# A graph network kernel: one gathered tile of every 64 moved from GpSimd to ScalarE's queue in three of six passes

## The reference

```python
h = relu(layernorm(x)); x = x + [(1 + eps) * h + segment_sum(h[src] * edge_weight, dst)]       # L0
h = relu(layernorm(x)); x = x + L1(h)   # h = relu(h @ W_node + b); 3 times: m = h @ conv[i],
                                        # agg = segment_sum(w_e * m[src], dst), h = GRU(agg, h)
h = relu(layernorm(x)); x = x + L2(h)   # segment_sum(alpha[rel] * (h @ w_rel)[src], dst) + ..., relu
h = relu(layernorm(x)); x = x + L3(h)   # (h + mean over src of h[dst]) @ W.T + b
```

## Time and profile before

| | us |
|---|---|
| median of 3 runs | 6545.01 (6538.51 to 6546.88) |
| profiled execution | 6555.57, of which the span is 6553.8 |
| POOL busy | 4766.0 (73%) |
| DVE busy | 3827.2 (58%) |
| PE busy | 3315.8 (51%) |
| ACT busy | 858.8 (13%) |

### The profile page before, as it was taken

The page is one execution under the profiler, slowest core; times in us unless marked ns, Lnnn a source line. Parts: engine busy times, 40 slices in busy tenths (PEclk is TensorE's granted clock), DMA queues, the critical chain, the costliest instruction groups (busy, mean ns, idle before and its releaser), DMA issues.

```text
span 6553.8 us, 107755 instructions
## 1 busy us (share of the span) xinstructions
PE 3315.8 (51%) x13560; PEld 2693.6 (41%) x13560; DVE 3827.2 (58%) x13371; ACT 858.8 (13%) x2167; POOL 4766.0 (73%) x5006
## 2 busy tenths in 40 slices
PE   3444445444447555555755554696444444444444
PEld 3333334333334444444444543343333333333333
DVE  6767666666666656656666664454454444444445
ACT  1000001000002111111211110143333333000000
POOL 6777776777774677777677777675777776777775
PEclk9555556555557666666876665696555555555556
DMA  5434442333332222222122222154222222222222
GB/s 140 111 107 110 110 110 74 74 75 75 75 75 53 53 54 54 54 54 53 46 54 53 53 54 54 48 212 140 54 53 54 53 54 55 54 54 54 54 54 59
DMA packets 276003, 471.96 MB, mean 72 GB/s; under 512 B 99701, under 2 KB 181882, under 8 KB 269035
## 3 DMA queue, kind: packets, MB, share of 16 engines
q0 software_dynamic: 156176, 306.05, 19.1%
q1 hardware_dynamic: 84091, 85.05, 3.8%
q10 hardware_dynamic: 35040, 73.87, 3.6%
HBM read 389.33 MB, written 77.27 MB: 71 GB/s over the span
## 4 chain that ended last, share of the span: by engine, by line
POOL 41%; issue 20%; DMA 13%; SPq 12%; PE 11%; DVE 3%; ACT 1%; DVEq 0%; POOLq 0%; ACTq 0%
POOL G L665 40%; DMA G<-h_rows,ix_src 11%; PE ps L769 10%; SPq L540 9%; SPq L532 3%; DMA G<-h_rows 1%; PE ps L826 1%; DMA t_rows<-G 0%; DVEq L1223 0%; DMA G<-t_rows,pos 0%; DVE HNA L1234 0%; SPq L551 0%; DVE bst L1151 0%; DVE M L1214 0%; ACT HG L1703 0%
## 5 line engine op out<-in xcount | busy, mean ns | idle before, releaser
L665 POOL DMA_INDIRECT G<-h_rows,ix_src x3860 | 3703.3, 959 | 1296.5 <-issue 1051.2
L769 PE MATMUL ps<-G,M 128*128 x10000 | 2554.6, 421 | 3081.0 <-SPq L551 2182.9
L769 PEld LDWEIGHTS ps<-G,M 128*128 128x128 f32 x10000 | 2168.9, 310 | 3431.6 <-issue 3425.9
L1234 DVE TENSOR_TENSOR HNA<-HNA,ps 128x128 f32 (+1 forms) x3328 | 957.8, 288 | 1359.8 <-PE ps L769 1338.8
L1214 DVE TENSOR_SCALAR M<-irow,rel,w_l 128x128 f32<-128x128 f32 x3328 | 1207.1, 365 | 180.7 <-issue 174.2
L665 POOL DMA_INDIRECT G<-t_rows,pos x770 | 740.9, 962 | 260.0 <-issue 228.8
L1234 DVE TENSOR_TENSOR HTA<-HTA,ps 128x129 f32 x840 | 243.3, 290 | 518.1 <-PE ps L769 509.7
L1803 ACT ACTIVATE sorting<-sorting,pk 128x128 f32<-128x128 f32 x784 | 250.6, 390 | 1446.9 <-DVE sorting L1409 1444.2
L769 PE MATMUL ps<-sorting 128*128 128x128 f32 x1568 | 435.1, 374 | 0.5 <-ACT sorting L1803 0.3
L1881 ACT ACTIVATE G<-G,pk 128x128 f32<-128x128 f32 x782 | 311.7, 402 | 679.1 <-DMA G<-t_rows,pos 678.7
L1234 DVE TENSOR_TENSOR X<-X,ps 128x128 f32 x832 | 239.1, 287 | 230.0 <-PE ps L769 223.6
(11 more groups left out here) (270 smaller groups left out, 2150.7 us busy)
## 6 DMA issues: line engine op xcount, KB each, us to landing
G<-h_rows SPq DMA_DIRECT2D x7680, 0.5 KB
G<-h_rows,ix_src POOLq DMA_INDIRECT x3860, 2.6
t_rows<-G SPq DMA_DIRECT2D x49, 1024.0 KB, 4.0
HTA<-in_edge_attr_n ACTq DMA_DIRECT2D x50, 500.0 KB
HTA<-in_edge_attr ACTq DMA_DIRECT2D x50, 500.0 KB
G<-t_rows SPq DMA_DIRECT2D x1536, 0.5 KB
sorting<-q_flat ACTq DMA_DIRECT2D x98, 196.0 KB
G<-t_rows,pos POOLq DMA_INDIRECT x770, 2.5
```

Source lines behind the costliest of these rows:

```text
L665: return nc.gpsimd.indirect_dma_start(to, None, table, bass.IndirectOffsetOnAxis(ap=ix, axis=0))
L769: return nc.tensor.matmul(dst, lhsT, rhs, start=start, stop=stop, skip_group_check=True)
L1234: V.tensor_tensor(to, to, ps[:, u % SLOTS, 0:n], ALU.add).then_inc(s_add, 1)
```

## The change

In PASS_L0, PASS_L1 and PASS_L3 the tiles with t % 64 = BY_ACT = 31, from t = 95 on (11 a pass, m = 1 to 11), are fetched by ACT, row by row: 128 DMAs of one row each, with row numbers from a new list act_by_one. They alternate between their own slot and a new one, RING + 1. In PASS_L0 ACT issues 64 rows in each turn of its chunk loop, in the first pass of L1 16 rows behind each load of Qb, and in PASS_L3 128 rows in one go, ahead of everything else. In the other passes POOL gathers these tiles as before.

SP waits for these tiles on semaphores of their own; its loop over three sets of four tiles of 64 is written out. `steps_of` has two chained DVE instructions more. rel_by_one now shares its place with starts and jump and is loaded after the last pass of L1; the list of relation keys of PASS_L3 is made for act_by_one too (two more short chained instructions of DVE in PASS_L2, and four more DMAs of SP ahead of it).

```diff
@@ slots
+def slot_of(t):
+    if t % (2 * RING) == RING + BY_ROW:
+        return RING
+    return RING + 1 if t % (2 * RING) == RING + BY_ACT else t % RING
@@ SP
-                with sp.Fori(0, ROW_SETS) as c:
+                for c in range(ROW_SETS):
...
+                    elif fetched_by_act(c * ROW_SET + t) and k in ACT_PASSES:
+                        m = c * ROW_PARTS + t // RING
+                        sp.wait_ge(s_rowa[k][m % 2], landed_by_act(m))
...
             sp.sem_inc(s_list1, 1)
+            sp.wait_ge(s_cix, NB)
+            list_rows(rel_by_one, "edge_type_16", BY_ROW, s_rel)
@@ POOL
-                    if t % RING != BY_ROW:
-                        gather(G[:, t % RING, 0:D], table, ix[:, t:t + 1]).then_inc(s_g[t % RD], 16)
+                    if fetched_by_pool(k, t):
+                        gather(G[:, slot_of(t), 0:D], table, ix[:, t:t + 1]).then_inc(s_g[t % RD], 16)
@@ DVE, steps_of
                 link(V.tensor_single_scalar(odd, to_b[at, :], 2 * RING - 1, ALU.bitwise_and))
-                link(V.tensor_single_scalar(odd, odd, RING + BY_ROW, ALU.is_equal))
                 link(V.tensor_single_scalar(to_b[at, :], to_b[at, :], RING - 1, ALU.bitwise_and))
-                link(V.tensor_tensor(to_b[at, :], to_b[at, :], odd, ALU.add))
+                for last, by in ((BY_ROW, 1), (BY_ACT, RING + 1 - BY_ACT)):
+                    link(V.scalar_tensor_tensor(to_b[at, :], odd, float(RING + last), to_b[at, :], ALU.is_equal, ALU.add))
+                    if by > 1:
+                        link(V.tensor_scalar(odd, odd, float(RING + last), float(by - 1), ALU.is_equal, ALU.mult))
+                        link(V.tensor_tensor(to_b[at, :], to_b[at, :], odd, ALU.add))
@@ DVE, ahead of PASS_L2 and in it
-            dve.wait_ge(s_ones, 16 * 2 * ROW_PARTS)
+            dve.wait_ge(s_rel, 16 * ROW_PARTS)
...
-            link(V.tensor_copy(rel_by_one[:], rel_by_one[:].bitcast(F32)))
-            link(V.tensor_single_scalar(rel_by_one[:], rel_by_one[:], 8, ALU.logical_shift_right))
+            for keys in (rel_by_one, act_by_one):
+                link(V.tensor_copy(keys[:], keys[:].bitcast(F32)))
+                link(V.tensor_single_scalar(keys[:], keys[:], 8, ALU.logical_shift_right))
@@ ACT
+            def rows_of_tile(k, m, part, parts):
+                c, j = divmod(m, ROW_PARTS)
+                if part == 0 and m >= 2:
+                    act.wait_ge(s_mm, k * S + (m - 2) * RING + BY_ACT + BLK)
+                n = P // parts
+                for e in range(part * n, (part + 1) * n):
+                    if (e - part * n) % RD == 0:
+                        regs = min(RD, n)
+                        _, row = nc.values_load_multi_w_load_instructions(
+                            act_by_one[32 * j:32 * j + 1, c * P + e:c * P + e + regs],
+                            ...
+                    act.dma_start(G[e:e + 1, BY_ACT if m % 2 == 0 else RING + 1, 0:D],
+                                  h_rows[bass.ds(row[(e - part * n) % RD], 1), :]).then_inc(s_rowa[k][m % 2], 16)
...
-            with act.Fori(0, EW_CHUNKS // 2 - 1) as i:
+            for i in range(EW_CHUNKS // 2 - 1):
+                if 1 + i // 2 < ROW_TILES:
+                    rows_of_tile(PASS_L0, 1 + i // 2, i % 2, 2)
                 for q in range(2):
                     act.wait_ge(s_ewc, 2 * i + q + 1)
                     ew_load(2 * i + 2 + q, q)
...
+                        elif j >= 2 and 1 + (j - 2) // 8 < ROW_TILES:
+                            rows_of_tile(PASS_L1, 1 + (j - 2) // 8, (j - 2) % 8, 8)
...
+            act.wait_ge(s_ix, 3)
+            act.wait_ge(s_hst, 16 * stores(N3))
+            for m in range(1, ROW_TILES):
+                rows_of_tile(PASS_L3, m, 0, 1)
```

More of the change, by code:

```diff
@@ L49 @@
 BY_ROW = RING - 1
+BY_ACT = RING // 2 - 1
 ROW_SETS, ROW_PARTS = 3, 4
@@ L90 @@
 PASS_PLACE = PASS_L1
+ACT_PASSES = (PASS_L0, PASS_L1, PASS_L3)
 PASS_ORDER = {PASS_L1 + 1: (0, 4), PASS_L1 + 2: (4, NB)}
@@ L191, in gnn_kernel @@
         one_by_one = sb("one_by_one", [P, ROW_SETS * P], I32)
-        rel_by_one = sb("rel_by_one", [P, ROW_SETS * P], I32)
+        act_by_one = sb("act_by_one", [P, ROW_SETS * P], I32)
         key_i = sb("key_i", [P, NB], I32)
@@ L231, in gnn_kernel @@
         c_pre = sb("c_pre", [BLK, NB])
-        starts = sb("starts", [P, NB, HB])
+        chunk_rows = sb("chunk_rows", [P, 2 * NB * HB])
+        starts, jump = [chunk_rows[:, k * NB * HB:(k + 1) * NB * HB].rearrange("p (b h) -> p b h", b=NB)
+                        for k in range(2)]
+        rel_by_one = chunk_rows[:, 0:ROW_SETS * P].bitcast(I32)
         shift = gate[:, 6 * BANK:6 * BANK + NB * HB].rearrange("p (b h) -> p b h", b=NB)
-        jump = sb("jump", [P, NB, HB])
         first3 = sb("first3", [P, BLK])
@@ L363, in gnn_kernel @@
         s_row = [[sem(f"s_row{k}_{q}") for q in range(2)] for k in range(3 + LAYERS)]
+        s_rowa = {k: [sem(f"s_rowa{k}_{q}") for q in range(2)] for k in ACT_PASSES}
         s_ones = sem("s_ones")
         s_ones3 = sem("s_ones3")
+        s_rel = sem("s_rel")
         s_list1 = sem("s_list1")
@@ L433, in of, with fetched_by_act, landed_by_act, fetched_by_pool @@
             return t[:, 0:tiles(g) * P]
-        def uses(u):
-            return len([t for t in range(u, EF, RD) if t % RING != BY_ROW])
+        def fetched_by_act(t):
+            return t % RING == BY_ACT and t >= RING
+        def landed_by_act(m):
+            return 16 * P * len(range(2 - m % 2, m + 1, 2))
+        def fetched_by_pool(k, t):
+            return t % RING != BY_ROW and not (fetched_by_act(t) and k in ACT_PASSES)
+        def uses(k, u):
+            return sum(fetched_by_pool(j, t) for j in range(k) for t in range(u, EF, RD))
         def nth_use(t):
@@ L504, in _, with list_rows @@
                     .then_inc(s_rows, 16)
-            for to, name in ((one_by_one, "src"), (rel_by_one, "edge_type_16")):
+            def list_rows(to, name, place, done):
                 tile = a[name][0:ROW_SETS * ROW_SET * P].rearrange("(c j t e) -> j c t e", c=ROW_SETS, j=ROW_PARTS, e=P)
                 for j in range(ROW_PARTS):
-                    sp.dma_start(to[32 * j:32 * j + 1, :].rearrange("p (c e) -> p c e", e=P), tile[j:j + 1, :, BY_ROW, :]) \
-                        .then_inc(s_ones, 16)
+                    sp.dma_start(to[32 * j:32 * j + 1, :].rearrange("p (c e) -> p c e", e=P), tile[j:j + 1, :, place, :]) \
+                        .then_inc(done, 16)
+            list_rows(act_by_one, "src", BY_ACT, s_ones)
+            list_rows(one_by_one, "src", BY_ROW, s_ones)
             def h_store(phase, src, ready, at):
@@ L548, in one @@
                         sp.wait_ge(s_row[k][j % 2], 16 * P * (c * (ROW_PARTS // 2) + j // 2 + 1))
+                    elif fetched_by_act(c * ROW_SET + t) and k in ACT_PASSES:
+                        m = c * ROW_PARTS + t // RING
+                        sp.wait_ge(s_rowa[k][m % 2], landed_by_act(m))
                     else:
-                        sp.wait_ge(s_g[t % RD], 16 * (k * uses(t % RD) + c * nth_use(ROW_SET + t % RD) + nth_use(t) + 1))
+                        sp.wait_ge(s_g[t % RD], 16 * (uses(k, t % RD) + c * nth_use(ROW_SET + t % RD) + nth_use(t) + 1))
                     sp.sem_inc(s_arr[k], 1)
-                with sp.Fori(0, ROW_SETS) as c:
+                for c in range(ROW_SETS):
                     for j in range(ROW_PARTS):
@@ L614, in _ @@
             sp.wait_ge(s_list1, 2)
-            for j in range(ROW_PARTS):
-                sp.dma_start(rel_by_one[32 * j:32 * j + 1, :].bitcast(F32).rearrange("p (x e) -> p x e", e=P),
-                             by_tile[j:j + 1, :, BY_ROW, :]).then_inc(s_ones3, 16)
+            for to, place in ((rel_by_one, BY_ROW), (act_by_one, BY_ACT)):
+                for j in range(ROW_PARTS):
+                    sp.dma_start(to[32 * j:32 * j + 1, :].bitcast(F32).rearrange("p (x e) -> p x e", e=P),
+                                 by_tile[j:j + 1, :, place, :]).then_inc(s_ones3, 16)
             for q in range(2):
@@ L774, in one_round @@
                     lists[ROW_SLOT:ROW_SLOT + 1, bass.ds(r * RD, steps)], engines=[mybir.EngineType.PE],
-                    min_val=0, max_val=RING,
-                    skip_runtime_bounds_check_because="a slot is a tile's number modulo RING, or RING itself")
+                    min_val=0, max_val=RING + 1,
+                    skip_runtime_bounds_check_because="a slot is slot_of a tile")
                 _, upto = nc.values_load_multi_w_load_instructions(
@@ L1108, in _ @@
             V.memset(one_by_one[:], 0)
-            V.memset(rel_by_one[:], 0)
+            V.memset(act_by_one[:], 0)
             V.memset(X[:, NN_FULL:NT, :], 0.0).then_inc(s_pad, 1)
@@ L1751, in ew_load @@
                 act.dma_start(za[:, q, 1, :, :], e_dram[:, at, :]).then_inc(s_ewl[q], 16)
+            def rows_of_tile(k, m, part, parts):
[8 more added lines that the diff above has]
```

(16 more changed lines are left out.)

12 lines of the change are left out of this document (6 added, 6 removed).

## The result

The changed kernel takes **6575.7 us** (median of 5 runs, 6573.7 to 6579.7) against 6545.0 us of the kernel before, measured beside it: ratio 1.0048, 95% interval 1.0037 to 1.0058. The forecast was 6506 us, with 0.07 on slower. The profiled execution has a span of 6577.6 us, 23.8 more than before.

A forecast was written before the change was run, and what follows sets the result against it. POOL's gathers were taken to bound each pass: 41.6 us saved by eleven fewer in three passes, plus 2.1 for steps_of, gives -39.5 us; from the 6545.0 median, 6506 us, forecast 6500 to 6514 (0.69), range 6496 to 6537.

The forecast's parts named there:

- the sentence on PASS_L0's chunk loads: PASS_L0: first buffer's load issued up to 14 us later, needed two chunks later; loads keep some 5 to 10 us.
- ACT's own work, 32.8 us a turn: PASS_L0, 32 steps: 64 rows 26.9 us, two register loads 4.3, four chunk loads with waits 1.6; 32.8 of 36.7 us.
- rival 1: ACT's queue becomes the bound from 0.48 us a row in L0: 6556 us, or 6900 at 0.62; chance 0.09.
- The rival's other half, L1: First L1 pass: ACT's piece exceeds 9.3 us from 0.475 us a row; at 0.50, +15 in place of -14 us.
- Rival 2: Late landings stall POOL on first tiles, 3 to 8 us each in L0 and L1, 1.5 in PASS_L2: 6520 us; chance 0.14.
- Eleven gathers from each pass: POOL runs free, so eleven gathers fewer save 13.8 us in L0, 14.0 in first L1, 13.8 in L3: 41.6 us.
- A row on ACT at 0.42 us, between 0.40 and 0.62: ACT's queue: cost of each one-row DMA, bounds 0.40 us (as SP) and 0.62 us, taken as 0.42.
- The rule on the shared descriptor block: Skill's rule that two sequencers lock it in turns: 0.45 us a row, ACT's L0 turn 34.7 of 36.7 us; doubted.
- Tile 95 of the first L1 pass 6.5 us late, tile 159 perhaps 4, POOL untouched: First L1 pass: late tiles hold SP and PE, but POOL keeps 9 us spare; costed at 0, at most 3 us.
- steps_of, +2.1 us at the start: Two new chained DVE instructions delay the first gather by 2.1 us; in PASS_L2 taken as 0, at most 1.5 us.
- Rival 3, longer gathers: POOL's gathers in the three passes grow, 0.01 us each making 23 us: 6535 us; chance 0.08.
- SP's arrivals written out: SP's loop written out takes three jumps a pass away, time SP has to spare; costed at nothing either way.

The follow-up runs named there:

- 112 + 13: Changed kernel with each PASS_L0 chunk load of 125 partitions issued as two, of 112 and 13 partitions: 6501.0 us, ratio 0.9939 to the kernel before.
- 115 + 10: Changed kernel with each PASS_L0 chunk load issued as two, of 115 and 10 partitions: 6562.8 us, ratio 1.0038 to the kernel before.
- in between: Changed kernel with ACT's PASS_L0 rows interleaved, 32 ahead of each chunk wait instead of 64 ahead of two: 6525.4 us, ratio 0.9976 to the kernel before.
- one load: Changed kernel with the second chunk load of each pair left out in PASS_L0 after the first two pairs: 6510.0 us, ratio 0.9949 to the kernel before.
- half the rows: Changed kernel with whole chunk loads, ACT fetching 32 rows a turn instead of 64 in PASS_L0 from m = 3: 6509.2 us, ratio 0.9954 to the kernel before.

## Why the prediction was wrong

**The step that failed** is the sentence on PASS_L0's chunk loads: "the load of the first chunk buffer is issued up to 14 us later than now, since the rows stand ahead of its wait ... the loads keep some 5 to 10 us." Its delay was right (with 112 + 13 the two buffers' loads stand 5.0 us apart in the median, not 18.1, so the first is some 13 us later), and so was ACT's own work, 32.8 us a turn: measured in the turn shown are 25.3 for the rows, 4.5 for two register loads and 2.4 for the chunk loads and what lies between, 32.2. Two things were taken as unchanged that the delay changes, and the turn of 32.8 us had no term for an issue that is held up, which measured some 8 us a turn.

- The delay removes the distance between the two chunk buffers. They were loaded 18.1 and 18.9 us apart (medians); with 64 rows ahead of both waits, both waits are over when ACT comes to them, and the pairs follow each other at 0.7 us and then 40.2.
- Two pairs at once back up. The first lands after 12.6 us, the second after 28.0, and an issue behind them is held for 5 to 10 us. Over PASS_L0 this makes 138.4 us of ACT's queue. From 290 us on it is 7.8 us a turn in issues of over 1 us, and 9.5 with the shorter ones in the turn shown. ACT needs 40.9 us a turn (mean of 21 turns, from the first load at 133.2 us to the one at 992.3) of 36.7.

From there it holds itself: ACT never waits, so the pairs stay together, so the next issue is held up. This is the prediction's **rival 1**, ACT's queue as the bound, but not with the price that it was given. There it took a row of 0.48 us or more; the row was 0.395 (0.42 forecast), and the missing time came from the hold-up instead. Its formula doesn't fit: with the measured turn it gives 22 x (40.9 - 37.3) - 5 = 74 us, and L1 began 57.6 us later. Two things are missing in it. A turn before the change was not 37.3 us but 36.7, twice the 18.3 of the earlier trace rows; so the loads fall behind by more, and the last load that has rows ahead starts 94 us later than before (992.3 against 898.1). And the last two turns have no rows, so there the loads catch up 30 us: the very last one starts 64.1 us later (1057.1 against 993.0), which less the 5 us of slack is the 59 us by which DVE's last add came later. The rival's other half, L1, didn't come.

**Rival 2** had the right place for the traffic. The earlier trace rows was read for the mean, 14.9% of 16 engines, and the prediction said itself that a mean can't tell which engines bear it. The trace has a way to tell, which I didn't use: count how many of the chunk loads' packets are under way at once. Before, it is five for 54% of the time in which there are any, and more than five for under 5%. With 112 + 13 it is most often sixteen, with 115 + 10 five again. The packets of four bytes that come with every DMA say it too. One row has one of them beside its 512 bytes (2274 packets for SP's rows, of which SP issued 1134 in that time). The loads, between 100 and 1000 us, have 5.0 each in the kernel before, 14.5 for each part with 112 + 13 and 7.3 with 115 + 10.

And in the changed kernel just one is under way for 20% of that time, against 5.5% before: one of the five ways is left with a tail. That fits with rows and chunk loads meeting on one engine, though the trace doesn't name the engines, so this last point stays inferred. Five ways at 14.9% x 16 / 5 are busy for 48%, not 15. The Trainium skill (DMA: Bandwidth & Descriptors, "Why a DMA increments its semaphore by 16 and not by 1") says that a transfer is spread over the largest number of engines up to 16 that divides the slowest dimension of both its sides, which for these loads is the partitions. Worked out from that, 125 and 115 give five, 112 gives sixteen, 13 and 10 give thirteen and ten. The trace agrees: (16 + 13) / 2 is the 14.5 above and (5 + 10) / 2 is near the 7.3, and the times of the 112 and 115 cuts agree too.

Rival 2's own mechanism, POOL held on the first tiles, with 3 to 8 us in L0, is seen at about its size: one wait for PE near 142 us, of 4.1 us in the changed kernel, 5.6 in between, 5.0 with one load, 5.4 with half the rows and 3.1 with 115 + 10, and none over 0.3 with 112 + 13 or without rows in L0. It isn't what makes the 58.

**Point by point, the rest:**

- *Eleven gathers from each pass*: right in the first L1 pass (14.1 us) and L3 (14.6). Most of the saving is there in L0 once ACT isn't the bound: 957.6 us with 112 + 13, 11.4 less than before (13.8 forecast), with gathers of 0.957 us instead of 0.954.
- *A row on ACT at 0.42 us, between 0.40 and 0.62*: about 0.395, just under the range. Register loads of 32: 2.24 us, against the 2.15 taken.
- *The rule on the shared descriptor block* did not show. In L1 and L3, with SP's rows beside them, ACT's issues take:

```profile
L1805 ACTq DMA_DIRECT2D G<-h_rows x1408: 227/235/550, 1192.3 to 2005.5; - x176
...
L1805 ACTq DMA_DIRECT2D G<-h_rows x1408: 223/224/522, 5571.8 to 6385.3; - x176
```

  A pair of issues in turns would need 0.45 us each, and ACT's rows came each 0.39. In L1, between 1140 and 2000 us, 920 of ACT's 1394 row issues overlap in time with one of SP's, and their median is 235 ns with or without. So two issues don't exclude each other for their whole length; the row that was to speak against the rule did so rightly.
- *Tile 95 of the first L1 pass 6.5 us late, tile 159 perhaps 4, POOL untouched*: counted from the pass's first arrival, tile 95 came 5.2 us later than before and tile 159 0.6. They came 7.8 and 4.3 us after the arrival ahead of them, where it was 2.2 and 1.1. PE stands there, and POOL's gap stays what it was:

```profile
1263.44 0.94 POOL L699 DMA_INDIRECT G<-h_rows,ix_src  x1 [0.31 <-issue]
1264.61 2.07 PE L803 MATMUL ps<-G,M 128*128 x8 [6.85 <-SPq L582]
```

- *steps_of, +2.1 us at the start*: the chain takes 9.8 us instead of 7.7, as worked out, but began 1.3 us earlier in this execution, so the first gather starts 1.0 us later (56.8 against 55.8); in the other kernels with the change it starts at 57.0 to 58.0. In PASS_L2 one gap of POOL is 1.3 us instead of 0.3, 3.1 us after PE resumes behind `steps_of`; that is 1.0 us, within the 0 to 1.5 given:

```profile
4877.85 0.95 POOL L699 DMA_INDIRECT G<-t_rows,pos  x1 [1.30 <-PE ps L803]
```

- *Rival 3, longer gathers*: 0.953 us in L0, 0.966 in L1, 0.946 in L3, all within 0.002 of before. It didn't happen in the changed kernel; with 112 + 13 it is 0.957 in L0, 0.003 more.
- *SP's arrivals written out*: 0, shown alone.

The sum of -39.5 us was itself sound: with the clog removed, the kernel with 112 + 13 takes 6501.0 us against 6539.8 beside it, 38.8 less. (The spans of the two profiled executions are 44.9 us apart, but those are single executions.) That the sum is met so closely is in part luck: in that kernel PASS_L0 gave 2.4 us less than its term and the first L1 pass 1.5 more.

**What stays open.** Whether the issue is held because a limited number of transfers may be outstanding on a queue, or for want of room for their descriptors, no run here tells apart. Nor is it known why the interleaved order stops at 38.1 us a turn: its hold-ups are 46 us, about 2 us a turn, and ACT's own 32.2; the rest would be the wait for DVE, which is itself late by the loads that take some 20 us with rows among them.

## What to carry to other kernels

When work is put ahead of a wait on a queue that also issues large transfers, don't ask only whether the queue has time enough: ask which transfers will now be issued together, and whether their path takes them at that rate. Read a DMA share of the page as a lower bound, and count how many packets of the transfer are in flight at once. If it is five of sixteen, the transfer is three times as full a pipe as the share says, and a small change of its partitions (125 to 112 + 13) may remove the clog for nothing.

## What the runs showed of the hardware that I had not expected

- An issue on ACT's queue can take up to 10.0 us, with no wait in the program, when four loads of 0.5 MB each were issued within 2.2 us ahead of it; the median is 0.235 us. The one held up can be a one-row transfer (changed kernel) or a chunk load (115 + 10: 9.3 us).
- The same 1 MB pair lands in 11.4 us as 125 partitions and in 5.8 as 112 + 13 (kernel before, nothing else changed), although a packet then takes longer, 244 ns against 179 in the mean.
- Transfers of one row on SP's queue start later behind chunk loads of ACT's queue: 1.6 us after the issue (median) in the kernel before, 5.9 in the changed one, 0.9 with the kernel before and 112 + 13. In L1 and L3, without chunk loads, ACT's rows start after 0.9 us.
